# A transformer block on eight cores: the store of y on another DMA queue, layer-norm loads with another wait, and a shorter ring of projection banks

## The reference

```python
x = x + attn(layernorm(x))        # low-rank q/k/v per head, 16 heads of 64, causal
x = x + ffn(layernorm(x))         # 1024 -> 4096, exact gelu, -> 1024

# attn, per head: q = rms(xh WqT), k = rms(xh WkT), v = xh WvT, each 64 wide,
# and 64 further columns q_r = q WQR, k_r = xh WKR
# softmax(q k^T / 8, causal) v, times W_O
# layernorm(x) = (x - mean) / sqrt(var + 1e-5) over the 1024 columns
```

## Time and profile before

| | us |
|---|---|
| median of 2 runs | 11281.33 (11276.04 to 11286.61) |
| the profiled execution | 11275.12 |
| its span, slowest core (core 7) | 11273.6 |
| spans of the 8 cores | 11249.4 to 11273.6 |
| busy on core 7: PE, DVE, ACT, POOL | 5913.1, 4850.2, 2675.0, 159.0 |

### The profile page before, as it was taken

One profiled execution on the slowest core, in us unless ns is written; L12 is line 12 of the kernel. 1 busy time (PEld: TensorE's weight loads), 2 busy tenths in 40 slices (PEclk: granted clock), 3 DMA queues, 4 the chain that ended last, 5 costly groups with the idle time before them and its releaser, 6 DMA issues.

```text
span 11273.6 us, 103735 instructions; the slowest of 8 cores (11249.4 to 11273.6 us)
## 1 busy us (share of the span) xinstructions
PE 5913.1 (52%) x29865; PEld 2738.3 (24%) x29865; DVE 4850.2 (43%) x16593; ACT 2675.0 (24%) x4510; POOL 159.0 (1%) x312
## 2 busy tenths in 40 slices
PE   3344545434454653344545434454653677677678
PEld 1112222211222222112222211222221333333333
DVE  4555555555555555555555555555551111111111
ACT  2222222122222222222222222222221112112111
POOL 0000000000000000000000000000000000000000
PEclk5555555555555555555555555555556888888889
DMA  0000000000000000000000000000004110110110
GB/s 18 19 2 17 2 17 2 17 19 1 19 2 18 1 2 17 19 2 17 3 17 2 17 19 1 18 2 16 1 1 82 38 35 22 38 33 24 38 34 26
DMA packets 63864, 192.32 MB, mean 17 GB/s; under 512 B 8808, under 2 KB 8848, under 8 KB 62288
## 3 DMA queue, kind: packets, MB, share of 16 engines
q0 software_dynamic: 42624, 117.46, 4.6%
q1 hardware_dynamic: 20688, 68.24, 1.9%
HBM read 168.89 MB, written 67.11 MB: 21 GB/s over the span
## 4 chain that ended last, share of the span: by engine, by line
PE 40%; DVE 34%; issue 13%; ACT 8%; DMA 2%; DVEq 1%; another core or an unknown queue 1%; ACTq 0%; POOL 0%; SPq 0%; POOLq 0%
DVE S_sb L737 7%; DVE PT L823 7%; PE ps_c L839 7%; PE pt_x L813 5%; PE pt_y L813 5%; PE ps_c L1052 4%; PE ps_b L1074 4%; PE ps_a L1074 4%; PE ps_d L1052 4%; DVE mcol L754 2%; DVE qn_tok L592 2%; DVE kst L618 2%; DVE S_sb L747 2%; DVE qst L521 2%; ACT P_B L784 2%
## 5 line engine op out<-in xcount | busy, mean ns | idle before, releaser
L784 ACT ACTIVATE P_A<-S_sb,negm,rstdq_win 128x256 bf16<-128x256 f32 (+15 forms) x512 | 661.4, 1292 | 3600.9 <-PE pt_y L813 2568.7
L839 PE MATMUL ps_c<-PT,vst 128*64 128x512 bf16 (+3 forms) x2560 | 733.9, 556 | 1189.2 <-DVE PT L823 1189.2
L724 PE MATMUL ps_s<-kst,qst 128*128 128x512 bf16 (+3 forms) x1280 | 655.5, 530 | 570.5 <-DVE S_sb L737 429.5
L823 DVE COPY PT<-pt_x 128x1024 bf16<-128x1024 bf16 (+1 forms) x640 | 407.9, 637 | 1012.3 <-PE pt_x L813 1011.9
L823 DVE COPY PT<-pt_y 128x1024 bf16<-128x1024 bf16 (+2 forms) x640 | 374.2, 585 | 1089.3 <-PE pt_y L813 1089.3
L737 DVE TENSOR_SCALAR_CACHE_REDUCE S_sb<-ps_s 128x512 f32<-128x512 f32 (+2 forms) x1152 | 673.6, 614 | 320.5 <-PE ps_s L724 294.2
L784 ACT ACTIVATE P_B<-S_sb,negm,rstdq_win 128x256 bf16<-128x256 f32 (+15 forms) x512 | 661.2, 1291 | 524.8 <-DVE negm L767 524.2
L813 PE MATMUL pt_x<-id_bf,P_A 128*128 128x128 bf16 x2304 | 358.3, 305 | 694.7 <-ACT P_B L784 673.8
L1085 DVE TENSOR_SCALAR ybf<-ps_a,b2col 128x512 bf16<-128x512 f32 x64 | 48.1, 751 | 1304.5 <-PE ps_a L1074 1304.5
L606 PE MATMUL pt_y<-id_bf,qn_tok 128*64 128x128 bf16 x1024 | 132.2, 311 | 883.4 <-DVE qn_tok L592 883.4
L839 PEld LDWEIGHTS ps_c<-PT,vst 128*64 128x64 bf16 x2560 | 204.2, 127 | 1492.8 <-issue 1492.8
(11 more groups left out here) (168 smaller groups left out, 9273.3 us busy)
## 6 DMA issues: line engine op xcount, KB each, us to landing
x_buf<-x SPq DMA_DIRECT2D x64, 512.0 KB, 7.5
x2s<-x_buf POOLq DMA_DIRECT2D x64, 512.0 KB, 6.0
x_buf<-x2s SPq DMA_DIRECT2D x64, 512.0 KB, 6.9
y<-x_buf POOLq DMA_DIRECT2D x64, 512.0 KB, 4.7
xln<-x POOLq DMA_DIRECT2D x64, 256.0 KB, 3.9
xln<-x2s POOLq DMA_DIRECT2D x64, 256.0 KB, 4.0
w1b<-W POOLq DMA_DIRECT2D x8, 1024.0 KB, 41.1
w2b<-W POOLq DMA_DIRECT2D x32, 256.0 KB, 78.1
```

The lines of the kernel that those rows point to most:

```text
L724: P.step("pe", lambda t, h=h, qt=qt, off=off, w=w, ps=ps: t.matmul(ps[:, 0:w], qstack[h][:, qt * 128:(qt + 1) * 128], kstack[h][:, off:off ...
L784: P.step("ac", lambda a, P_sb=P_sb, po0=po0, klen=klen, slot=slot, spar=spar, rc=rc: a.activation(out=P_sb[:, po0:po0 + klen], in_=S2[spar ...
L823: P.step("dv", lambda v, par=par, qt_min=qt_min: v.tensor_copy(PT2[par][:].rearrange("p (h f) -> p h f", f=512) [:, :, qt_min * 128:512], ...
L839: P.step("pe", lambda t, hi=hi, grp=grp, v0=v0, par=par, qt_min=qt_min, j=j, nj=nj: t.matmul(ps_c[hi * HD:(hi + 1) * HD, qt_min * 128:512] ...
```

## The change

Three things change.

1. In the projections the ring of PSUM banks has 4 entries instead of 6 (ps_s0 and ps_s1 leave it), and a unit goes to `w2_stage2` when 3 are queued instead of 5.
2. In `emit_ln2` the load of xln waits for its buffer and for the spills of attention (a fixed count of f_x2, noted once as `SPILLS`), not for the stores of y so far. The square on ACT waits for a noted count of dv_f, that of `varb` of the chunk before (`sq_guard`), not for the row sum just ahead of it.
3. The 4 stores of y at the end of an FFN window are issued by SP instead of POOL. In SP's list they stand ahead of the reload of x2_buf for the next window, which waits for them as before. POOL's list has only the loads of xln left in this stage.

```diff
@@ -484,8 +484,7 @@
                     rot4 = [(ps_a, r_psa), (ps_b, r_psb),
-                            (ps_c, r_psc), (ps_d, r_psd),
-                            (ps_s0, r_ps0), (ps_s1, r_ps1)]
+                            (ps_c, r_psc), (ps_d, r_psd)]
@@ -632,7 +631,7 @@
-                                ps, r_ps = rot4[uidx[0] % 6]
+                                ps, r_ps = rot4[uidx[0] % 4]
@@ -649,7 +648,7 @@
-                                if len(pendu) >= 5:
+                                if len(pendu) >= 3:
                                     w2_stage2(*pendu.popleft())
@@ -961,9 +960,11 @@
             WCAST = d_g.n
+            SPILLS = f_x2.n
 
             prev_w2_end = 0
             ln2_marks = {}
+            sq_guard = [0]
@@ -973,7 +974,7 @@
                     P.step("po", lambda g, row0=row0, par=par: g.dma_start(
                         out=xln[par][:], in_=x2s[row0:row0 + 128, :]),
-                        wait=[f_xl[par], (st_out, st_out.n)],
+                        wait=[f_xl[par], (f_x2, SPILLS)],
                         inc=d_xl[par], inck=16)
@@ -982,7 +983,8 @@
                     P.step("ac", lambda a, par=par: a.activation(
                         out=xn2[:], in_=xln[par][:],
                         func=AF.Square, accum_out=sqsum[:]),
-                        wait=[(d_xl[par], ld), dv_f] + r_xn2.waits(),
+                        wait=[(d_xl[par], ld), (dv_f, sq_guard[0])]
+                        + r_xn2.waits(),
                         inc=ac_f)
@@ -994,6 +996,7 @@
                         wait=[ac_f, dv_f], inc=dv_f)
+                    sq_guard[0] = dv_f.n
@@ -1113,7 +1116,7 @@
-                    P.step("po", lambda g, b=b, t0=t0, tc=tc: g.dma_start(
+                    P.step("sy", lambda sy, b=b, t0=t0, tc=tc: sy.dma_start(
                         out=y_out[b, t0:t0 + 128, :],
                         in_=x2_buf[:, tc * D:(tc + 1) * D]),
                         wait=[(dv_f, add_done)] if tc == 0 else [],
```

## The result

| | before | changed kernel |
|---|---|---|
| median, us | 11281.6 (10 runs) | 11002.3 (11 runs) |
| profiled execution, us | 11275.1 | 11002.3 |
| its slowest core, span | core 7, 11273.6 | core 0, 11000.7 |
| ratio, 95% interval | | 0.9739 [0.9705, 0.9772] |

The forecast was 10979.5 us with a range of 10955 to 11022.

What follows compares the result with a forecast made beforehand. No engine was full; waits between engines, in the FFN's window-change bubbles, were what counted. Savings of 247.4 (loads), 47.6 and 6.8 (square), 301.8 us in all, took 11281.3 to 10979.5 us; range 10955 to 11022.

Steps and rivals of the forecast that it cites:

- Loads of xln: FFN window changes: loads no longer wait for the stores of y, removing 247.4 us of idle time in 14 waits.
- Square: FFN layer norms: ACT's square no longer waits for musum, saving 0.85 us per chunk, 47.6 plus 6.8 us.
- What is late next: FFN bubble: loads for the third and fourth chunks have 7.1 us to land, median 5.4; no loss taken.
- collision rival: FFN bubble: xln loads collide with stores and reload, third chunk 1.9 us late, 27 us in all, 11006; chance 0.15.
- First matmuls: After each FFN bubble: the clock still falls to 0.50, so the first matmuls stay as slow; no gain.
- Projections: Head of each attention window: 4 banks instead of 6 and 2 groups ahead instead of 4 cost 0.
- The tail: End of the run: last stores go out on SP, bounds -1 to +3 us once, taken as 0.

Runs made afterwards that it cites:

- e6: Changed kernel with four xln buffers instead of two, so all four loads go out in the bubble before; median 10983.7 us, ratio 0.9741.
- e5: Changed kernel, but SP's reload of x2_buf waits until the bubble's layer norms are done; runs took 11040 to 11353 us, core 0 about 10971.0.
- e4: Changed kernel, but the xln loads wait for the stores of y again, which stay on SP; median 11220.8 us, ratio 0.9941.
- e3: Changed kernel, but POOL issues the stores of y again; xln loads only stand behind their issue; median 11152.3 us, ratio 0.9884.
- e1: Kernel before with only the projection change: 4 banks instead of 6, 3 queued instead of 5; ratio 1.0012.
- e8: Changed kernel with the next window's layer norms placed inside the second matmuls of a window; runs of 10656.4 to 10929.9 us, ratio 0.9487.
- e9: Kernel before with only the stores of y moved from POOL to SP; six fastest runs 11267.7 to 11275.8 us, ratio 0.9970.
- e10: Kernel before with only the square's wait changed, run once more for an undisturbed profile; 11217.4 us in one run.
- e7: Changed kernel, but the last window's stores of y go out on POOL with their own semaphore; median 11018.3 us.

## Why the prediction was right, and what it missed

The sum, from the first `musum` of the FFN to the end of the span:

| | us | measured |
|---|---|---|
| before, core 7 (8596.80 to 11273.6) | 2676.8 | |
| less `musum` behind the stores, 14 bubbles | -247.4 | none left before a first chunk |
| less the square, 64 chunks | -54.4 (forecast) | 0.84 a chunk, 53.8 |
| plus the tail | +6.3 | |
| sum, with no late chunk | 2381.3 | e6: 2381.5 (core 4); e5: 2380.4 (core 0) |
| plus the fourth chunk's load, core 0 | +20.4 | |
| sum | 2401.7 | changed kernel: 2404.1 (core 0) |

*Loads of xln: right in mechanism and size.* The full 247.4 us went from before the first chunk, and e4 and e3 show that it takes both the dropped wait and the empty POOL queue, as the step said. A detail was off: the loads for the next bubble go out one by one (10282.31 and 10290.02 in the bubble shown), not as a pair.

*Square: right.* 0.85 us a chunk, DVE's own chain next: 5.72 us where 5.71 was forecast, 6.89 where 6.88.

*What is late next: the step that failed.* Its times of issue were exact (5.5 and 11.1 us after the adds), and its landing time was not. It took the median of 5.4 us for both loads. That held for the third chunk, whose load went out before the reload began and landed in 5.6 us. The fourth chunk's load goes out into the reload, as the step itself said, and yet it got the same median; there it landed in 9.1 us, and 7.3 were to be had (10276.59 to 10283.85). The median mixed 28 loads that ran alone (3.4 to 4.3 us) with 28 beside the reload (6.6 to 11.9), and no load took it; the right row was the one with the same neighbour, the 8.96 us of the earlier trace rows. The reload began 7.5 us after the adds and not 9, but at 9 it would have stood beside a load issued at 11.1 just as well. The step cost 20.4 us on core 0 (12.2 on core 7). The collision rival priced this at 27 us (11006) and is the nearest to what happened, but it put the lateness on the third chunk and argued that the fourth would then be in time. The Trainium skill, "DMA: Bandwidth & Descriptors", section "Issuing engines are not separate DMA queues", says that DMAs started by different engines run on the same 16 DMA engines. The trace agrees: the load from POOL's queue took 9.1 us beside SP's reload and 3.4 to 4.3 alone. The estimate of 3.2 us from the Trainium skill, "DMA: Bandwidth & Descriptors", section "Anatomy of one DMA — SWDGE (gpsimd) path", was never reached; the least was 3.4 us before and 3.5 after.

*First matmuls: right.* 5.67 us from the first group to the third, 5.82 before: the clock fell in the shorter bubble too (0.51 from 10266 to 10290, 0.54 from 10290.6 to 10294).

*Projections: right.* e1 finds no change beyond a few us.

*The tail: bounds too narrow.* -1 to +3 us were given and +6.3 came. The step looked at how long a transfer takes, but the data were as quick as before; the time is after them, and its cause is open.

Forecast 10979.5, plus 20.4, plus 6.3 gives 11006; the median is 11002.3. Both misses go the same way and do not cancel. That the time still lies within the range is owed to its upper end, which had been set for a collision of up to 3 us per bubble; the one that came cost 1.5 on core 0.

## What to carry to other kernels

When a wait goes, time the next DMA against what runs beside it at that moment, and take its landing from rows with the same neighbour, not from the median of the line. A load that must run ahead needs both its wait and its queue free; either alone brings a part at most. And a bubble made of a chain that nobody needs yet is better moved under work of an engine that is idle there (e8: 25 us a window) than shortened.

## What the runs showed of the hardware

- A kernel whose SP stores to DRAM in the FFN ends 15.5 to 16.9 us after its last adds (changed kernel, e4 to e9, all cores), one whose POOL does all stores 9.3 to 9.4 us (before, e1, e3, e10), though the last data move as fast. The queue of the last stores alone does not decide it (e7). The cause is open.
- In dense FFN windows there were stretches at a mean granted clock of 0.81 instead of 1.00: in e8 some 1100 us on cores 0 and 1 and 200 us on core 5 of the same run, and a window then takes 146.5 instead of 122.7 us. The Trainium skill, "TensorE: Matmul & The Clock Gate", section "Seeing it yourself", tells of a limiter that takes a whole die to 13/16 once three of its cores run dense matmuls, and holds it while the load lasts. The trace agrees in the level (0.81). It does not agree in the other two: while cores 0 and 1 were at 0.81, cores 2 and 3 of the same die were at 1.00 under the same work, and from about 9800 on it was the other way round. What sets off such a stretch no run here shows.
- A load of 256 KB in bf16 landed in 3.4 to 4.3 us where nothing else of size ran (before, core 7), in 6.6 to 11.9 us beside a reload of 2 MB before, and in 7.5 to 9.5 us beside it in the changed kernel (core 0).
